# Query norms by matmul and memory, layer-norm columns by GpSimd, and another order of TensorE's queue in a fused delta-rule and mixture-of-experts kernel

## What is computed

```python
x = x + attn(layernorm(x)); x = x + moe(layernorm(x))
# attn, with x normalized:
q, k, v = (silu(causal_conv4(x @ W)) for W in (Wq, Wk, Wv))   # 8 heads of 64
q = q * rsqrt(sum(q * q, per head) + 1e-6); k likewise; q *= 64 ** -0.5
beta = sigmoid(x @ Wb)
# per token: u = beta * (v - k.S);  S += k u^T;  o = q.S
o = o * rsqrt(mean(o * o, per head) + 1e-5) * norm_w
attn = o @ Wo
# moe: gate over 16 experts (4 groups, 2 kept, top 4), SwiGLU experts of 352,
# and a shared SwiGLU of 704 for all tokens
```

## Time and profile before

| | |
|---|---|
| median of 3 runs | 1263.47 us (1261.1 to 1267.51) |
| the profiled execution's own time | 1262.86 us |
| its span, first to last instruction | 1261.1 us |
| TensorE busy (matmul) | 1223.0 us, 97% |
| VectorE busy | 839.0 us, 67% |
| ScalarE busy | 365.3 us, 29% |
| GpSimd busy | 349.6 us, 28% |
| attention part | 0 to about 550 us |
| mean granted clock of TensorE | 0.99 |

### The profile page before, as it was taken

One profiled execution on the slowest core, in us unless ns is written; L12 is line 12 of the kernel. 1 busy time (PEld: TensorE's weight loads), 2 busy tenths in 40 slices (PEclk: granted clock), 3 DMA queues, 4 the chain that ended last, 5 costly groups with the idle time before them and its releaser, 6 DMA issues.

```text
span 1261.1 us, 26634 instructions
## 1 busy us (share of the span) xinstructions
PE 1223.0 (97%) x8779; PEld 750.5 (60%) x8779; DVE 839.0 (67%) x2340; ACT 365.3 (29%) x804; POOL 349.6 (28%) x417
## 2 busy tenths in 40 slices
PE   8999989999998999999999999999999999999995
PEld 7887767877776656544444455555555555555553
DVE  5897688769869573344420377777877777777773
ACT  4755645655553323220000011111111111111111
POOL 3411324322332122212564112122222222221222
PEclk9999999999997999999999999999999999999998
DMA  5444953843563396255546777888888887879762
GB/s 169 88 60 98 142 122 78 161 114 86 114 143 128 89 240 139 93 194 192 193 169 245 246 172 179 207 185 221 185 208 200 230 189 175 209 176 235 181 141 26
DMA packets 214307, 202.43 MB, mean 161 GB/s; under 512 B 72608, under 2 KB 154528, under 8 KB 214176
## 3 DMA queue, kind: packets, MB, share of 16 engines
q1 hardware_dynamic: 130080, 112.25, 35.5%
q10 hardware_dynamic: 67456, 54.24, 16.7%
q0 software_dynamic: 16640, 34.24, 13.1%
HBM read 123.76 MB, written 81.08 MB: 162 GB/s over the span
## 4 chain that ended last, share of the span: by engine, by line
PE 55%; DMA 0%; DVE 0%; issue 0%; POOLq 0%; ACT 0%; DVEq 0%
PE pD L2491 13%; PE pG L2478 12%; PE pU L2478 12%; PE pD L2459 4%; PE pG L2440 4%; PE pU L2440 4%; PE pD L2488 2%; PE pG L2474 2%; PE pU L2474 2%; PE pU L2434 1%; PE pD L2454 1%; DMA out<-front_region,ix 0%; DVE ups L2366 0%; POOLq L2161 0%; ACT front_region L2311 0%
## 5 line engine op out<-in xcount | busy, mean ns | idle before, releaser
L2366 DVE STREAM_TRANSPOSE ups<-a 32x96 f32<-32x96 f32 (+1 forms) x1136 | 296.6, 261 | 35.3
L2239 POOL DMA_INDIRECT out<-front_region,ix x64 | 99.3, 1552 | 355.5 <-DMA out<-front_region,ix 169.7
L2491 PE MATMUL pD<-w,ups 128*128 (+1 forms) x384 | 176.5, 595 | 0.7 <-DVE ups L2366 0.7
L2478 PE MATMUL pG<-w,xsT 128*128 x512 | 162.7, 460 | 0.0
L2478 PE MATMUL pU<-w,xsT 128*128 x512 | 161.9, 459 | 0.0
L1010 PE MATMUL pProj<-front_region 128*128 128x256 f32 x624 | 153.8, 389 | 2.2 <-ACT front_region L742 1.6
L2478 PEld LDWEIGHTS pG<-w,xsT 128*128 128x128 f32 x512 | 96.2, 189 | 74.1 <-issue 32.9
L2478 PEld LDWEIGHTS pU<-w,xsT 128*128 128x128 f32 x512 | 97.3, 190 | 54.2
L1010 PEld LDWEIGHTS pProj<-front_region 128*128 128x128 f32 x624 | 112.5, 190 | 20.0 <-ACT front_region L742 2.0
L2491 PEld LDWEIGHTS pD<-w,ups 128*128 128x128 f32 (+1 forms) x384 | 72.0, 190 | 78.9 <-issue 67.9
L2301 ACT ACTIVATE g<-pG 128x352 f32<-128x352 f32 x72 | 33.4, 463 | 285.8 <-issue 120.8
(11 more groups left out here) (327 smaller groups left out, 1804.2 us busy)
## 6 DMA issues: line engine op xcount, KB each, us to landing
w<-in_expert_T SPq DMA_DIRECT2D x80, 384.0 KB
front_region<-in_expert_T ACTq DMA_DIRECT2D x64, 352.0 KB
slot_rows<-zeros SPq DMA_DIRECT2D x72, 266.0 KB, 7.4
front_region<-slot_rows ACTq DMA_DIRECT2D x288, 64.0 KB
front_region<-in_expert_T ACTq DMA_DIRECT2D x32, 256.0 KB
front_region<-in_L_attn_hidden_states SPq DMA_DIRECT2D x16, 256.0 KB, 3.8
x2r<-in_L_attn_hidden_states SPq DMA_DIRECT2D x16, 256.0 KB, 4.4
partial_sums<-x2r SPq DMA_DIRECT2D x16, 256.0 KB, 3.3
```

Of the source, the lines that this page charges most:

```text
L2239: pool.indirect_dma_start(out=flat, out_offset=bass.IndirectOffsetOnAxis(ap=to[:, 0:1], axis=0), in_=y[(q - 1) % RING][:, :], in_offset=No ...
L2366: dve.transpose(aT[par][B * to:B * to + B, 0:n, rows], a[rows, 0:len(IC) * P].rearrange("p (c n) -> p c n", c=len(IC))[:, 0:n, B * to:B * ...
L2478: mm = pe.matmul(out[:, 0:I], rows[:, k, :], w[:, bass.ds(weights[0], 1), 2 * I * k + at:2 * I * k + at + I], start=(k == 0), stop=(k == D ...
L2491: return pe.matmul(out[:, :], gated_[0:m, c, :], w[0:m, bass.ds(weights[0], 1), at:at + D], start=(c == 0), stop=(c == 2))
```

## The change

Five things, all in the attention part.

1. *Columns of x.* The kernel gets a second input `x_T`, x already turned by the host. For the pairs from 2 on (`TURNED` = 2) the turns `xT`, `make_xn` and `xnT_copy` are gone. SyncE loads the raw columns straight into `xnT` (512 KB), stores the per-token numbers `r1` and `nm1` to memory (`store_rows1`), and loads them back to all 128 partitions (`spread_rows1`, into `xin[0]`). GpSimd multiplies and adds in place (`scale_columns`). VectorE's statistics still read the rows that `load_x` brings.
2. *Query lengths.* The turns `qT` and VectorE's `q_sums` are gone. ScalarE squares the queries as they lie, two instructions a pair; TensorE sums 64 partitions at a time by matmul with a matrix of ones and zeros (`q_lengths`: four matmuls of 256 columns a pair, 32 output partitions each, at partitions 0 and 32); ScalarE copies the sums out (`q_copy`), SyncE stores them and loads them back turned, in four DMAs of 4-byte elements.
3. *Order of TensorE's queue.* `merge_x` stands right behind `hop_r`; `betas` moves from slot 0 to slot 1 behind the gate; the second `kT` of a pair from slot 1 to slot 2 (`late_turn`); `merge_w` to the end of slot 5.
4. *A bank more.* The first chunk of each slot 0 projects into `pG` (`ahead_of_scores`), for which it waits for what the scores wait for, and `hop_u_and_scores` waits for ScalarE's copies of that chunk (`first_chunk`).
5. *ScalarE's order.* `w_copy` and `x_copy` stand directly behind `raw_copy` or ahead of it; `route["tri"]`, whose memory lends room to the query sums, is filled by GpSimd in tile 12.

The core of the diff:

```diff
+            def load_columns(p):
+                sp.wait_ge(s_proj, place(p - 2, 3 * DC - 1) + 1)
+                sp.wait_ge(s_bp, p - 1)
+                sp.wait_ge(s_xnT, 2 * p)
+                sp.dma_start(xnT[p % 2][:, :, :], xTp_d[p].rearrange("p (c n) -> p c n", c=DC)).then_inc(s_xcl, 16)
+            def store_rows1(p):
+                sp.wait_ge(s_xcl, 48 * (p - TURNED) + 16)
+                sp.wait_ge(s_r1, p + 1)
+                sp.dma_start(rows1_d.rearrange("o (p n) -> (o p) n", n=4), rows1[:, :]).then_inc(s_xcl, 16)
+            def spread_rows1(p):
+                sp.wait_ge(s_xcl, 48 * (p - TURNED) + 32)
+                sp.dma_start(xin[0][:, :], rows1_d.to_broadcast([P, P * 4])).then_inc(s_xcl, 16)
+            def store_q_sums(p):
+                sp.wait_ge(s_qc, p + 1)
+                least(sp, s_qss, 80 * p)
+                sp.dma_start(qs_d, qsT[:, :]).then_inc(s_qss, 16)
+            def load_q_sums(p):
+                sp.wait_ge(s_qss, 80 * p + 16)
+                least(sp, s_qe, p)
+                for i in range(2):
+                    for f in range(2):
+                        sp.dma_start(ssq[:, H * i + HH * f:H * i + HH * f + HH],
+                                     qs_d[B * f:B * f + HH, P * i:P * i + P].rearrange("r n -> n r"),
+                                     allow_slow_non_contiguous=True).then_inc(s_qss, 16)
...
+                    if even and s == (4 if u == -4 else 1) and TURNED <= (u + 8) // 2 < PAIRS:
+                        load_columns((u + 8) // 2)
+                    if not even and TURNED <= (u + 7) // 2 < PAIRS:
+                        if s == 1:
+                            store_rows1((u + 7) // 2)
+                        if s == 2:
+                            spread_rows1((u + 7) // 2)
+                    p = (u + 3) // 2
+                    if not even and pair_ok(p):
+                        if s == (3 if p == 0 else 2 if p == PAIRS - 1 else 1):
+                            store_q_sums(p)
+                        if s == (4 if p in (0, PAIRS - 1) else 2):
+                            load_q_sums(p)
...
+            def scale_columns(p):
+                pool.wait_ge(s_xcl, 48 * (p - TURNED + 1))
+                both = xnT[p % 2][:, :, :].rearrange("p c (i n) -> p c i n", n=P)
+                link(pool.tensor_tensor(both, both, by_token(0), ALU.mult))
+                pool.tensor_tensor(both, both, by_token(1), ALU.add).then_inc(s_xnT, 2)
...
+                    if s == 3 and even and pair_ok((u + 2) // 2):
+                        q_coefs((u + 2) // 2)
+                    if s == 3 and not even and TURNED <= (u + 7) // 2 < PAIRS:
+                        scale_columns((u + 7) // 2)
...
             def project(g, u=None):
...
-                least(pe, s_raw, 2 * g if g >= EARLY else 2 * g - 2)
+                if ahead_of_scores(g):
+                    scores_wait(u + 1)
+                    pe.wait_ge(s_PT, u + 1)
+                else:
+                    least(pe, s_raw, 2 * g - 2 if g < EARLY or ahead_of_scores(g - 1) else 2 * g)
...
-            def qT(t):
...
+            def q_lengths(p):
...
+                for n in range(2):
+                    for f in range(2):
+                        mm = pe.matmul(pT0[B * f:B * f + B, 0, 0:PW], heads[:, 2 - 2 * n:2 - 2 * n + B], sq[f][:, cols(n, PW)],
+                                       start=(n == 0), stop=(n == 1))
+                mm.then_inc(s_qtp, 1)
...
+                    if s == 0 and tile_ok(u):
+                        merge_x(u)
                     if even and pair_ok(pk):
-                        project(3 * DC * pk + s)
+                        project(3 * DC * pk + s, u)
```

More of the change, by code:

```diff
@@ L327, in chunk @@
         return p, i + DC
+    TURNED = 2
     EARLY = 9 * DC
@@ L892, in _ @@
                         o_copy(u - 1, 1)
+                    if tile_ok(u) and s == 0 and u < FUSED:
+                        x_copy(u)
                     if even and pair_ok(pk):
@@ L905, in _ @@
                             shared_silu(n)
-                    if tile_ok(u) and s == 0 and u < FUSED:
-                        x_copy(u)
-                    if even and s == (0 if pk else 1) and pair_ok(pk) and pk != 1:
+                    if s == 5 and tile_ok(u + 1):
+                        w_copy(u + 1)
+                    if even and s == 1 and pair_ok(pk) and pk != 1:
                         tanh(pk)
@@ L929, in _ @@
                         silu(3 * DC * old + 11)
-                    if even and s in (2, 3) and old == 1:
-                        q_squares(s)
+                    if even and s == 2 and old == 1:
+                        q_squares(1)
                     if even and s in ((4, 5) if old in LATE else (3, 5)) and pair_ok(pk):
@@ L1362, in _ @@
                         vT_turn(opening(u, s) - 14)
-                    if opening(u, s) in (18, 19):
-                        qT(opening(u, s) - 18)
+                    if opening(u, s) == 19:
+                        q_lengths(0)
                     if s == 0:
-                        if tile_ok(u):
-                            merge_x(u)
                         if u + 3 == NT - 2:
-                            qT(NT - 1)
-                        if even and pair_ok(pk) and pk > 1:
-                            betas(pk)
+                            q_lengths(PAIRS - 1)
                         if not even and pair_ok(pq) and pq != 1:
@@ L1374, in _ @@
                     if s == 1:
-                        if not even and pair_ok(pq) and pq != 1:
-                            kT(2 * pq + 1)
                         if tile_ok(u - 3):
                             gate(u - 3)
+                        if even and pair_ok(pk) and pk > 1:
+                            betas(pk)
+                    if s == late_turn(u) and not even and pair_ok(pq) and pq != 1:
+                        kT(2 * pq + 1)
                     if s == 2:
@@ L1381, in _ @@
                             x2T(u - 2)
-                        if even and pair_ok(old) and 0 < old < PAIRS - 1:
-                            (vT_turn if old in LATE else qT)(2 * old)
+                        if even and pair_ok(old) and old in LATE:
+                            vT_turn(2 * old)
                         if even and old == PAIRS - 1:
@@ L1392, in _ @@
                             oT_turn(u - 1)
-                        if even and pair_ok(old) and 0 < old < PAIRS - 1:
-                            (vT_turn if old in LATE else qT)(2 * old + 1)
+                        if even and pair_ok(old) and old in LATE:
+                            vT_turn(2 * old + 1)
+                        elif even and pair_ok(old) and 0 < old < PAIRS - 1:
+                            q_lengths(old)
                         if even and old == PAIRS - 1:
                             vT_turn(2 * old + 1)
-                        if not even and pair_ok(new) and new != 1:
+                        if not even and new == 0:
                             xT(2 * new)
@@ L1401, in _ @@
                             out_proj(u - 1)
-                        if even and pair_ok(old) and 0 < old < PAIRS - 1:
-                            (qT if old in LATE else vT_turn)(2 * old)
-                        if not even and pair_ok(new) and new != 1:
+                        if even and pair_ok(old) and 0 < old < PAIRS - 1 and old not in LATE:
+                            vT_turn(2 * old)
+                        if not even and new == 0:
                             xT(2 * new + 1)
@@ L1736, in _ @@
                             make_v(2 * old + s - 3)
-                        if s == 5 and old in LATE:
-                            q_sums(2 * old)
-                        if s in (3, 4) and 0 < old < PAIRS - 1 and old not in LATE:
-                            q_sums(2 * old + s - 3)
                         if s == 1 and old == PAIRS - 1:
@@ L1756, in _ @@
                         make_v(2 * ((u + 3) // 2) + 1)
-                    if not even and s == 0 and (u + 3) // 2 in LATE:
-                        q_sums(2 * ((u + 3) // 2) + 1)
-                    if u + 3 == NT - 2 and s in (1, 2):
-                        q_sums(NT - 3 + s)
                     if (u, s) == (FIRST, SLOTS - 1):
@@ L1774, in _ @@
                         make_v(opening(u, s) - 14)
-                    if opening(u, s) in (19, 20):
-                        q_sums(opening(u, s) - 19)
                     if s == 3 and late_gram(u - 1):
```

208 lines of the change are left out of this document (115 added, 93 removed).

## The result

The changed kernel takes 1288.75 us (median of 4 runs, 1285.42 to 1292.29), the kernel before 1265.0 beside it (1261.1 to 1267.51): ratio 1.0198, 95% interval 1.0172 to 1.0225, so 2% slower. The prediction said 1284, with a range of 1275 to 1297. The profiled execution of after took 1292.29 (span 1290.3, granted clock 0.975 of full), that of before 1262.86 (span 1261.1, clock 0.990): 29.4 us between the two. The runs differ by up to 7 us among themselves, so the profile after shows some 3.5 us more than the median does.

A forecast was written before the change was run, and what follows sets the result against it. TensorE, busy 97% of the span, was taken to bound the kernel. From the profiled 1262.86 us, 22.8 for the stop, 3 for the clock and -4.9 of later gains gave 1283.8, with 0.6 to the median 1284; range 1275 to 1297.

The forecast's parts named there:

- The stop: At tile 0's first projection, TensorE waits for pair 3's columns behind SyncE's 18 loads: 22.8 us later, bounds 17.5 and 27.
- The anchor: Start of the stop's chain: VectorE's copy ending the first inverse at 93.63, pair 3's numbers ready at 94.05; no shift taken.
- The clock: TensorE's clock under 1 behind the stop at tile 0: 3 us in the sum, 2 to 5 in the range.
- The later gains: Tiles after the stop get shorter through order, betas, x turns, query lengths and VectorE's saving: -4.9 us in sum.
- term for borders: TensorE's queue, 10 tiles: one run of small tiles less between 128x128 groups, 0.2 us per tile, -2.0 in all.
- VectorE's saved `q_sums`: At the ends of tiles 2 and 6, two q_sums of 0.68 us less per tile shorten waits for `x2r`: -2.6.
- The queries' part: Query lengths by matmul on TensorE cost +1.3 us over six pairs; VectorE's saving gives -2.6; SyncE's small loads 0.
- The saved x turns: TensorE, slot 4: 0.43 us saved for each of 4 turns left after the stop, -1.7; those in slot 3 save nothing.
- Rival 2: GpSimd's scaling blocks VectorE, 3.2 us per pair, felt in tiles 3 and 7: 1290 us; chance 0.09.
- Rival 4: TensorE's matmuls for query lengths are not packed: each costs 0.87 us more, +5, 1289 us; inside the range.
- Rival 3: SyncE held in tiles 1 to 7, so a further pair is late by some 15 us: 1300 us; chance 0.08.
- Rival 1: Pair 3's rows reach GpSimd by about 100 us, row store issued before 93, no stop: 1257 us; chance 0.06.

The follow-up runs named there:

- rows_early: The changed kernel with SyncE's store and spread of pair 3's rows moved to slot (-1, 0), ahead of the inverse loads of tiles 1 to 3: 1270.55 us, ratio 1.007.

## Why the prediction was right, step by step

- **The stop: right in place and cause, 4 us short.** Predicted 22.8, measured 26.8. Its terms: the row store at 116.84, measured 119.30; the two landings with the issue between them 6.3, measured 6.2 (1.5 for the store, 4.8 for the spread); the two GpSimd instructions 4.4, measured 5.8. Together 2.5 - 0.1 + 1.5, and 127.5 becomes 131.4. The size that I took for 128x1024 from twice a 128x512 of 1.09 was the wrong end of a range that I had not given: alone it took 2.85, 2.6 times as much for twice the elements.
- **The anchor: a wrong step.** I took no shift of VectorE's first inverse and held pair 2's stall to be swallowed by this stop. The inverse came 5.9 us later, 5.2 of it through GpSimd's two instructions (94.69 without their length), each known to 2 or 3 us. GpSimd held VectorE in two places and TensorE waited 5.81 for pair 2, and what VectorE does after that feeds the stop; a stall ahead of a stop is swallowed only if the stop's chain doesn't start behind it. That SyncE was quicker after it (the 18 loads in 9.7 us from 109.58 on, where they took 12.0 with the long gaps of before, and 1.2 less ahead of them) gave 3.4 of the 5.9 back. With the rows early the stop is still 12.4 us.
- **The clock: 3, measured 2.6.** No run shows the 3 that stands in the sum, or the 2 and the 5 of the range: they were my estimates, the 3 from the program's first 36 matmuls, which take 6.81 us where turns at 0.43 / 4 each would take 3.9, and the profile has a granted clock of 1.00 there (0 to 8 us). What the runs show of the clock beside a stop: in the changed kernel, where TensorE stands from about 114.5 to 131.4, it was 1.00 in 115 to 116 us, 0.65 in 116 to 117 and 0.50 in 117 to 136; in the kernel before it was 0.50 in 399 to 410, after a wait of 1.97 us that ended at 396.33. The 2.6 is a difference of two kernels: between the first projection and `hop_u` of tile 0 lie 6.28 us, in the kernel without columns 3.65. The first projection took 3.58 from start to start instead of 1.83, at the clock of 0.50, and this is TensorE's stretch around it in the changed kernel (stretch, its length, busy us and instructions, granted clock, DMA share, GB/s):

```profile
120.00:140.00 20.00, 8.57 (x90) 0.58 0.64 109
```

- **The later gains: -4.9, measured -6.1** (tiles 3 and 7 aside), but by other parts than I had, so that the sum is near by luck. The order alone was sized at -2.4 and measures -5.5. Its term for borders, -2.0, came out at some -1.8 from twice as many borders at half the price; the rest is the waits for `x2r` in tiles 2 and 6, which I had put down to VectorE's saved `q_sums` (-2.6) and which the order removes with `q_sums` in place. The queries' part was sized at -1.3 and measures 0 by itself and +0.8 to +2.8 beside the order; its transfers on SyncE, which I took at 0, are the likely reason and not more than that. The saved x turns were sized at -1.7 and, with the loads of columns that replace them, measure nothing. The packed 1.07 us for the queries' sums was 0.99.
- **Rival 2 came true beside the forecast, not in its place.** I had priced GpSimd's hold at +6 in two tiles and gave it 0.09. Against before it is 2.9 + 4.5 = 7.4, against the kernel without columns 9.7. My range for one tile, up to 4, held the 2.9 and not the 4.5, in which the clock fell too. I held it to be unlikely on 3.2 us of hold a pair and a slack of 1.7; the rows of tile 3 have 3.9 us of hold and a wait of 2.84, so a slack of about 1.0. How long one instruction can be held, the rows of pair 2 show: a step of 0.45 us took 3.08 beside an instruction of 3.00.
- **The sum.** 26.8 + 0.7 to `hop_u` of tile 0 (2.6 of clock less what order gave there) + 7.4 - 6.1 = 28.8, the shift of tile 14. With 1262.86 that is 1291.7, the profiled time within 0.6. The forecast of 1284 is 4.8 under the median, and it is as near as that by luck: errors of 4.0 and 7.4 in the loss met 1.2 more gain, a clock term taken in full where only 0.7 net was seen, and runs 3.5 us faster than the profiled one. As a ratio it was 1.0162 (over 1263.47), under the interval that was measured, 1.0172 to 1.0225. The lower end of the range was also mis-added: its terms (17.5, 2, 4.9 and 1) give 1277, not 1275.
- **Rival 4** (sums not packed) is refuted at its mechanism: 0.99 against 1.85 us. (The sign that I had for it compared 64 columns with 128: like for like, with half a turn's 0.107 for 64 columns as an estimate, the grams' 0.69 us stand against 1.7 and not 3.4, which still says the same.) **Rival 3** (a further pair late by 15) did not occur: no later pair's columns were waited for. **Rival 1** was tried as `rows_early`: the row store was issued at 102.40 there and not before 93, so its stop of some us stayed, and with pair 2's stall it is still 0.7% slower than before.

Open: four issues of zeros in tile 1 take 4.4 us of SyncE in the kernel without columns (from 129.52) and 6.0 in the changed one (from 140.54), where one elsewhere takes 0.53, which moves what follows by a few us; why, and how much of the queries' part it makes, wasn't tried. Nor was the wait of 8.0 us for the sums' landing.

## What to carry to other kernels

Where a step goes from engines to the DMA queue, look at what stands ahead of it in that queue at the one time it is needed: here 18 loads of another tile, and moving two issues ahead of them gave back 16 of 25 us. A stall hides inside a later stop only if the later stop's chain starts from something the stall did not delay. And price work moved to GpSimd by what VectorE does in those microseconds: 5.8 us a pair of GpSimd, an engine that had been busy for 28% of the time, cost 7.4 us in four pairs. Last, count a wait for a landing in a queue of issues as work of that queue: here 8.0 us of it stood beside 2.0 us of loads.

## What the runs showed of the hardware

- A GpSimd product or sum of 128x1024 with one operand at a stride of 4 elements took 2.85 us alone and up to 3.69 beside VectorE (columns from pair 4 on; up to 3.68 in the changed kernel), and one of 128x512 1.05; VectorE's instruction that met it grew from 0.45 to 3.08, from 0.31 to 2.75 and from 1.22 to 3.79, while a reduction of 128x1024 beside the second of GpSimd's instructions kept its 1.22.
- Eight matmul instructions of 256 columns on 128x32 tiles took 0.99 us when they went to two groups of 32 columns, in either order of issue, and 1.85 when all went to one: a factor of 1.87 for two groups.
- A load of 128 rows by 4 elements of 4 bytes, turned, kept SyncE for 0.5 us, so four of them for 2.03.
- From issue to landing a store of 2 KB took 1.7 us with the rows early and 10.6 behind the stores of zeros in tile 1 (columns from pair 4 on), and one of 64 KB 11.4 there (no columns).
